# A two-layer cross-attention on one core: layer-1 denominators gathered ahead of the query stack, layer-0 values stored ahead of keys and output, x1 rounded in one cast

## The reference, cut to what matters

```
# layer 0, 8 heads of 40; enc = context rows 0..72, ca = the last 4 rows
query, keyt, valt = x @ Wq, enc @ Wk, enc @ Wv
hs = mha(query, keyt, valt)                       # softmax over 73 keys
ca_q1 = einsum('btc,th->bch', ca, Wq_ca)[:, indices, :]   # 192 channels, spread to 256 rows
ca_hs1 = mha(ca_q1, x, x)                         # attends to x itself
ca_hs2 = mha(ca_hs1 @ Wq, ca @ Wk_ca, ca @ Wv_ca) # softmax over 4 tokens
x1 = (hs + ca_hs2) @ Wout + b_out + x
# layer 1, 20 heads of 16, 77 keys
q, k, v = x1 @ Wq, ctx @ Wk, ctx @ Wv
out = softmax(q k^T / 4) v @ Wo + bo + x1
```

## Time and profile before

| | |
|---|---|
| time, median of 3 runs | 376.36 us (375.27 to 383.32) |
| the profiled execution | 375.7 us, of which 373.9 us are its span |
| mean granted clock of TensorE | 0.939 |
| PE, DVE, ACT, POOL busy | 89%, 51%, 43%, 32% |
| DMA, share of 16 engines | 52.7% |
| HBM read, written | 37.38 MB, 19.10 MB |

### The profile page before, as it was taken

How to read it: one execution, slowest core, us unless ns; L and a number is a source line. 1 busy time by engine, 2 the same in 40 slices (tenths; PEclk the granted TensorE clock), 3 DMA queues, 4 the chain that set the end, 5 groups by cost and what they waited for, 6 DMA issues and landing times.

```text
span 373.9 us, 7987 instructions
## 1 busy us (share of the span) xinstructions
PE 333.4 (89%) x3044; PEld 255.1 (68%) x3044; DVE 189.4 (51%) x432; ACT 162.6 (43%) x343; POOL 121.0 (32%) x124
## 2 busy tenths in 40 slices
PE   3999589999989899989998999799989998696795
PEld 2777357678658777876777687668776866466545
DVE  4570104862763567267626852684368436214552
ACT  3434263316643564627263727272737172411320
POOL 4845050315043504540454045404541223204010
PEclk9999799999987999999999999999999999758956
DMA  8997925715276537654765476447654852123101
GB/s 245 265 354 275 240 77 148 177 31 162 76 198 171 172 107 182 182 185 116 183 181 195 121 182 198 156 136 181 187 166 134 196 187 87 34 39 128 42 2 42
DMA packets 39244, 57.38 MB, mean 153 GB/s; under 512 B 9888, under 2 KB 29128, under 8 KB 39208
## 3 DMA queue, kind: packets, MB, share of 16 engines
q1 hardware_dynamic: 39208, 56.88, 52.7%
HBM read 37.38 MB, written 19.10 MB: 151 GB/s over the span
## 4 chain that ended last, share of the span: by engine, by line
PE 43%; DMA 23%; DVE 13%; SPq 12%; issue 5%; ACT 3%; POOL 1%; DVEq 0%
DMA den<-u 7%; DMA q_scratch<-q 4%; PE bank L676 4%; DVE negm L954 4%; DMA u0b_scratch<-u 4%; DVE negmc L954 4%; PE bank L635 3%; PE bank L491 2%; PE bank L478 2%; PE bank L551 2%; DMA q0s<-mt 2%; PE bank L770 2%; PE bank L584 2%; PE bank L788 2%; PE bank L563 2%
## 5 line engine op out<-in xcount | busy, mean ns | idle before, releaser
L824 ACT ACTIVATE prob<-bank 77x512 f32<-77x512 f32 (+1 forms) x96 | 41.4, 528 | 23.9 <-PE bank L553 23.8
L1224 POOL TENSOR_TENSOR at0lo<-atu,at0hi 120x512 fp32r<-120x512 f32 x8 | 15.4, 1919 | 101.6 <-ACT at0hi L814 101.6
L954 DVE TENSOR_REDUCE negm<-bank 128x5 f32<-128x385 f32 (+2 forms) x88 | 42.2, 547 | 4.5 <-PE bank L804 4.5
L913 ACT ACTIVATE prob<-bank 73x512 f32<-73x512 f32 x32 | 16.4, 592 | 51.6 <-PE bank L752 51.6
L954 DVE TENSOR_REDUCE negmc<-bank 128x2 f32<-128x512 f32 x48 | 29.4, 680 | 7.1 <-PE bank L563 7.1
L1232 POOL TENSOR_TENSOR xlo<-x,xhi 128x256 fp32r<-128x256 f32 x16 | 11.4, 736 | 60.5 <-DVE xhi L1113 60.5
L814 ACT ACTIVATE q<-bank 120x512 fp32r<-120x512 f32 (+3 forms) x32 | 15.7, 491 | 33.7 <-PE bank L482 33.5
L551 PE MATMUL bank<-q,kp 32*77 32x256 f32 x320 | 25.1, 397 | 3.1 <-DVE x L1006 1.5
L1117 DVE TENSOR_TENSOR atu<-atu,rb 128x768 f32<-128x768 f32 x7 | 6.7, 960 | 39.4 <-DMA rb<-rec_scratch 35.5
L788 PE MATMUL bank<-prob,xkeys 128*64 128x192 f32 x256 | 24.3, 331 | 1.8 <-DVE negm L954 1.1
L1161 POOL TENSOR_TENSOR cast<-ca,small 96x1536 fp32r<-96x1536 f32 x8 | 22.0, 2752 | 11.7 <-PE bank L758 11.4
(11 more groups left out here) (175 smaller groups left out, 862.6 us busy)
## 6 DMA issues: line engine op xcount, KB each, us to landing
q_scratch<-q SPq DMA_DIRECT2D x8, 720.0 KB, 4.9
q0s<-q_scratch SPq DMA_DIRECT2D x8, 720.0 KB
xt<-in_xt SPq DMA_DIRECT2D x8, 384.0 KB, 5.1
u_scratch<-u SPq DMA_DIRECT2D x8, 384.0 KB, 3.2
out_t<-x SPq DMA_DIRECT2D x8, 384.0 KB, 4.3
q0s<-q_scratch SPq DMA_DIRECT2D x8, 360.0 KB
xkeys<-in_xkeys SPq DMA_DIRECT2D x8, 352.0 KB, 4.3
rbc<-recc_scratch SPq DMA_DIRECT2D x16, 144.0 KB, 2.6
```

Of the source, the lines that this page charges most:

```text
L824: nc.scalar.activation(p1[:, h:h + n, :].rearrange("p h q -> p (h q)"), ps_of("SC1", j, d)[0:KEYS1, 0:n * SQ], ACT.Exp, scale=SCALE1)\
L913: nc.scalar.activation(p0[:, 2 * j:2 * j + 2, :].rearrange("p h q -> p (h q)"), ps_of("SC0", j, b)[0:KEYS0, :], ACT.Exp, scale=SCALE0)\
L954: return nc.vector.tensor_reduce(out=out, in_=in_, axis=AX, op=ALU.max, negate=True)
```

## The change

Four edits. (1) SP gathers den1 ahead of the loads of the query stack, and so waits for the PV1 copies there; the four stores of u1 stay behind the stack. (2) SP issues den0 and the two stores of u0 ahead of `load_k0s` and `store_out`. (3) DVE forms x1 by three adds from PSUM, as before, then waits for them and makes x1hi by one cast of the whole x1 in SBUF, in place of three more adds from PSUM; POOL subtracts x1lo in one piece of 128x512 behind that cast, in place of two of 128x256 behind the single adds. (4) On POOL `build_cast(b + 1)` comes behind the at1 subtractions.

```diff
@@ SP
+                if s3 and d < LAST:
+                    drained(sp, "PV1", d, 0, 1, 2)
+                    sp.dma_start(den1[:, :], u1[D1:128:32, :, :]).then_inc(den1_in, 16)
                 if s1:
                     sp.wait_ge(q_st, 16 * (b + 1))
                     rows = q_d.rearrange("(h d) v n -> (d v) h n", d=D0)
...
                 if s3 and d < LAST:
-                    drained(sp, "PV1", d, 0, 1, 2)
-                    sp.dma_start(den1[:, :], u1[D1:128:32, :, :]).then_inc(den1_in, 16)
                     for s in range(4):
                         sp.dma_start(u1_d[s].rearrange("j d q -> d j q"), u1[32 * s:32 * s + D1, :, :]).then_inc(u1_st, 16)
...
                     load_xt(b + 1)
-                    load_k0s(b + 1)
-                if s4:
-                    store_out(e)
...
                     sp.dma_start(den0[:, :], u0[D0:128:64, :, :]).then_inc(den0_in, 16)
                     sp.dma_start(u0_d, u0[:, 0:3, :].rearrange("p j q -> p (j q)")).then_inc(u0_st, 16)
                     sp.dma_start(u0b_d, u0[:, 3, :]).then_inc(u0_st, 16)
+                if b + 1 < B:
+                    load_k0s(b + 1)
+                if s4:
+                    store_out(e)
+                if s1:
                     sp.wait_ge(rec0_ready, b + 1)
@@ DVE
-                        tt(x1[c % 3][:, m, :], ps_of("O", m, c)[:, 0:SQ], xt[c % 2][:, m, :], ALU.add)
-                        tt(x1hi[:, m, :], ps_of("O", m, c)[:, 0:SQ], xt[c % 2][:, m, :], ALU.add).then_inc(free_of("O", m, c), 1)
+                        tt(x1[c % 3][:, m, :], ps_of("O", m, c)[:, 0:SQ], xt[c % 2][:, m, :], ALU.add).then_inc(free_of("O", m, c), 1)
+                    drained(dve, "O", c, 0, 1, 2)
+                    cp(flat(x1hi), flat(x1[c % 3])).then_inc(x1hi_ready, 1)
@@ POOL
                 if s2:
-                    for m in range(2):
-                        drained(pool, "O", c, m)
-                        tt(x1lo[:, m, :], x1[c % 3][:, m, :], x1hi[:, m, :].bitcast(f32), ALU.subtract).then_inc(x1lo_step, 1)
-                    pool.wait_ge(x1lo_step, 2 * (c + 1))
-                    drained(pool, "O", c, 2)
+                    pool.wait_ge(x1hi_ready, c + 1)
+                    tt(flat(x1lo), flat(x1[c % 3])[:, 0:2 * SQ], flat(x1hi)[:, 0:2 * SQ].bitcast(f32), ALU.subtract).then_inc(x1lo_step, 1)
+                    pool.wait_ge(x1lo_step, c + 1)
                     tt(x1hi[64:128, 2, :], x1[c % 3][64:128, 2, :], x1hi[64:128, 2, :].bitcast(f32), ALU.subtract).then_inc(x1lo_ready, 1)
                     pool.wait_ge(x1lo_ready, c + 1)
-                if b + 1 < B:
-                    is_full(pool, "CT", 5, b)
-                    build_cast(b + 1)
                 if 0 <= d < LAST:
                     pool.wait_ge(at1hi_ready, d + 1)
...
                     pool.wait_ge(at1lo_ready, d + 1)
+                if b + 1 < B:
+                    is_full(pool, "CT", 5, b)
+                    build_cast(b + 1)
                 if b + 1 < B:
                     split_x(b + 1)
```

More of the change, by code:

```diff
@@ L270, in xattn_kernel @@
         k0s_in = [sem(f"k0s{i}_loaded") for i in range(2)]
-        xhi_ready, xlo_ready, x1lo_ready = (sem(n) for n in ("xhi_ready", "xlo_ready", "x1lo_ready"))
+        xhi_ready, xlo_ready, x1hi_ready, x1lo_ready = (sem(n) for n in ("xhi_ready", "xlo_ready", "x1hi_ready", "x1lo_ready"))
         kbd0_ready, cast_ready = sem("kbd0_ready"), sem("cast_ready")
```

## The result

The changed kernel takes 403.12 us (median of 4, 401.83 to 407.19), the kernel before 377.84 beside it: a ratio of 1.071, 95% interval 1.059 to 1.084. Slower, by 7%. The profiled execution has a span of 402.4 against 373.9 us.

A forecast was written before the change was run, and what follows sets the result against it. PE, 89% busy, was taken as bounded by each slot's chain of den1, den0 and maxima, nearly tied with POOL's path to Q. Waits of 23.1 plus 3 for the clock on 375.7 gave 401.8, forecast 402, range 384 to 416.

The forecast's parts named there:

- The stack starts late and SC0 waits: SP's query stack loads: start 1.4 us later in slot 5, land up to 8.1 behind issue; SC0 stalls 1.2 us.
- The u1 stores hold SP: SP before the first atu1 load: stores behind the stack land 1.2 us later in slot 5, and at1hi with them.
- The cast loses its cover: POOL between at1hi and Q: build_cast's 2.8 us less slack, so 1.9 to 2.8 us in each of slots 2 to 6.
- Slot 2: Slot 2: stack slips 4.3 us, stores cost 3.7 and the cast 2.8, together 6.5; PE stands about 4 before Q.
- The clock: PE's granted clock: one fall, in slot 2 behind the stall before Q, taken at 3 us of up to 6.5.
- the fall in every slot: Rival at 414, chance 0.20: in slots 3 to 6 PE's stalls each bring 6 us at 1.2 GHz, 12 us on top.
- The Trainium skill's price for a transfer: DMA of the stack: about 2.0 us plus bytes/436e3, landing 4.5 us after issue, so SC0 and the stores feel nothing.
- den0: Layer-0 denominator gather on SP: lands some 2 us sooner, worth nothing once POOL's path ends later than M1's old start.
- One cast for x1hi: VectorE's x1hi: gains only the two CT stalls on PE, 0.3 us a slot, set against SC0's stall.
- Slot 7: Slot 7: no cast and no split, but late u1 stores hold at1hi, rec0 and the maxima, + 1.4 us.
- short queue: Rival at 387, chance 0.18: the stack is late for nothing and the u1 stores land by their own issue; total 11 us.
- early at1hi: Rival at 372, chance 0.15: u1 stores land early with SP freed sooner, at1hi comes at 232.6, 0.7 us won per slot.

The follow-up runs named there:

- e8: e3 plus SP waiting for the PV1 copies ahead of the query stack loads, den1 gather still behind them; 381.5 us, ratio 1.020 to the kernel before.
- e1: Changed kernel with build_cast back ahead of the at1 subtractions on POOL; 390.8 us, ratio 1.029 to the kernel before.
- e2: Changed kernel with the den1 gather back behind the query stack loads, cast still late; 386.6 us, ratio 1.026 to the kernel before.
- e5: Kernel before with only build_cast moved behind the at1 subtractions; 382.7 us, ratio 1.027 to the kernel before.
- e9: Changed kernel with build_cast one step later still, behind split_x(b + 1) on POOL; 389.2 us, ratio 1.036 to the kernel before.
- e3: Changed kernel with den1 back behind the query stack and build_cast back ahead of the at1 subtractions; 366.7 us, ratio 0.968 to the kernel before.
- r1: The kernel before, unchanged, run again for a second profile; 371.8 us.
- e6: Kernel before with only den0 and the u0 stores moved ahead of the k0s loads and output store; 369.7 us, ratio 0.982 to the kernel before.
- e11: e3 run again in five rounds; 367.1 us, ratio 0.978 to the kernel before.
- e10: Kernel before with only the single cast for x1hi; 375.8 us, ratio 1.001 to the kernel before.
- e7: e3 with the den1 gather issued by ScalarE on its own DMA queue after the PV1 copies; 367.4 us, ratio 0.982 to the kernel before.

## Why the prediction was right, and where only its sum was

The forecast was 402 and the time 403.1, but the closeness is partly luck: the slots cost 9 us more than I had counted, and the end was 6.5 us cheaper. The waits were about right: 23.1 us forecast, and PE stands 20.2 us longer in slots 2 to 7. The clock was not: 3 us forecast, and PE is busy 15.1 us longer.

- *The stack starts late and SC0 waits.* Right. Forecast 1.2 us a slot and SC0 at up to 8.1 us behind the issue; measured stalls of 1.7 to 1.9 in slots 3 to 7 and 2.9 in slot 2. The 8.1 holds with the wait alone (e8: 8.0 to 8.4 in slots 3 to 7). I had not counted that the gather ahead makes it 8.7.
- *The u1 stores hold SP.* Right, and nearly in size: from the issue of the stack to the first atu1 load 9.6 us (240.62 to 250.22), forecast 9.1 (217.95 to 227.04). at1hi is cast 8.7 us behind that load, forecast 9.3. Counted from M1, though, at1hi is cast 2.8 us later than before in the mean of slots 3 to 6 (2.2 in e1), for 1.2 to 1.4 in the sum: the stack left 1.9 us later, not 1.4, and in slots with a fall more comes on top.
- *The cast loses its cover.* Right in slots 3 to 6: at1hi to the end of POOL 7.1 us, as forecast, with Q behind it. e1, e2, e5 and e9 show it from four sides. Worked out at 1.9 to 2.8 us in five slots it should give 10 to 14 us; the waits of PE that come with it in the profiled executions are 12 us alone (e2 against e3) and 10 on top of den1. The whole cost in the slots is 20, since PE's matmuls are in flight 8 to 10 us longer beside them.
- *Slot 2.* Right in size, wrong in its way. 6.5 us of waits, with PE standing 4 us before Q, and 3 for the clock were forecast; it came at + 8.4, of which PE's idle time is 2.2 and its longer busy time 6.2. SC0's 2.91 us are its longest stall, none stands ahead of Q, and the cast, given 2.8 there, cost 0.5 (e1).
- *The clock.* The term that was mis-sized. I took one fall, 3 us, for slot 2 and gave the fall in every slot 0.20 as a rival of 414. In the profiled execution it fell in every one of slots 2 to 6. Slots 3 to 6 last 171.1 us, where 145.4 + 15.2 = 160.6 were forecast: PE's idle time there grew by 16.9, near the 15.2, and its busy time by 8.7, for which I had nothing. The rival's mechanism was there, at 2.2 us a slot for its 3. That the time is nonetheless not 414 is the end: the profile that I built on had the longest of all, at 0.74.
- *The Trainium skill's gate rule* ("TensorE: Matmul & The Clock Gate", "Why this matters for your kernels"), an idle gap between bursts brings the lower rate back, was a better guide than my 0.20. The trace agrees at Q, 3.15 us of idle ahead of 266.13 and a granted clock of 0.66 from 266 to 271. But falls also stand behind SC0's shorter stalls, 1.82 us in slot 4 and 1.89 in slot 5, while those of 1.92 in slot 6 and 1.71 in slot 7 have none. *The Trainium skill's price for a transfer* ("DMA: Bandwidth & Descriptors", "Anatomy of one DMA"), by an estimate 4.5 us for the stack from a fit on the other kind of queue, does not fit: 8.1 in e8, with the core's own other traffic beside it.
- *den0.* In the changed kernel it wins nothing, as forecast: DVE's wait for it is 0.17 us in slot 5. Its price alone, up to 0.9 us a slot, was too small for the times. Slots 2 to 7 of e3 (M1 from 96.03 to 308.55, 212.5 us) are 4.7 us shorter than in the first profile of before, which would fit, but 8.7 shorter than in r1, and the medians say 8 to 13 us (e6, e11, e3). The clock doesn't explain it: r1 has a mean of 0.956 and e3 0.957, and e3's span is 7.0 us shorter. Which wait gives the rest stays open.
- *One cast for x1hi.* Right: nothing (e10).
- *Slot 7* was forecast at + 1.4 and came at + 1.3.

The rivals: *short queue* is out by SC0's stalls and by L358; *early at1hi* is out, since the reciprocals were early (246.01) and the stores were not.

## What to carry to other kernels

A small transfer moved ahead of a large one also moves its wait ahead: what is queued behind that wait on the issuing engine is the price. Here the largest load of the slot left 13.1 us behind M1 in slots 3 to 7, for 11.2 in the kernel before, for data that nobody needed yet. An operation that fills a gap on a slow engine should be moved only with the question of what follows it there; e9 shows that one place further on it was free again. A new stall on a nearly busy TensorE costs its own length and, where the clock falls with it, the slower matmuls too: 20 us of waits came with 15 of those. And when a sum is built on one profiled execution, look whether each part of it is typical: the end of this one was the longest of fourteen, its slots 4 us shorter than in a second execution, and its total hid both.

## What the runs showed of the hardware that I had not expected

- A gather of 20 KB issued on ScalarE's own queue, 1.5 us behind 1080 KB on SP's, landed 6.7 us after its issue (e7, slot 5), hardly sooner than behind them in the same queue (5.3 us from an issue 3.1 us behind the earlier trace rows): 8.3 and 8.4 us behind the first load.
- The same gather ahead of the stack makes the stack 0.6 us slower in slot 5 (8.72 for 8.12 us, e1 and e8), 0.5 in the mean of slots 3 to 7.
- The clock fell within 1 us of stalls of 1.8 to 1.9 us (slots 4 and 5 of after), and not with two others of that length (slots 6 and 7).
- The clock of one kernel that isn't changed ranged from 0.919 to 0.960 in its mean over the runs, and its time from 369.3 to 383.8 us.
